# A graph layer on one core: PE's sums in two banks by turns, half of its signals taken out, and two bias rows moved off PE

## The chip, the cores and the metric

The kernel runs on one core of a Trainium2 chip. The metric is the device time of one execution in microseconds (us): the median of three runs. Engines are named as in the profile: PE (matmul), PEld (its weight loads), DVE (vector), ACT (scalar), POOL (GpSimd), SP (sync, which here only issues DMAs).

## What is computed

One message-passing layer over 6250 nodes (128 features) and 100000 edges sorted by destination, with H = 256 hidden columns:

```
h    = relu(concat(x[src], x[dst]) @ Wm1 + bm1)
h    = relu(h @ Wm2 + bm2)
agg  = segment_sum(h @ Wm3 + bm3, dst) / clip(count, 1)
upd  = relu(concat(x, agg) @ Wn1 + bn1) @ Wn2 + bn2
out  = layernorm(x + x + upd)
```

The kernel keeps near float32 accuracy by splitting an operand into a high and a low part ("hi", "lo") and multiplying the parts separately.

## The kernel before, in words

**Opening stage** (up to about 90 us). For each of 13 groups of four windows (a window is 128 nodes), PE transposes x (L1066) and multiplies it by the two halves of Wm1 (L1084) and by half of Wn1 (L1105). A one-row matmul (L1078) puts the bias bm1 into the bank of the first product. ACT copies the first product (table a, L555) and the high half of the second (table b, L562); DVE makes b's low half (L836). ACT adds bn1 to one half of the Wn1 product (L566) and DVE to the other (L841). DVE works out from the edges the words and flags that steer the loop (L741 to L795), each a row of 392 numbers. Both tables go to DRAM.

**Edge loop** (about 95 to 1358 us). The 391 blocks of 256 edges run four to a body (U = 4); bodies 0, 1 and the last are written out, the others are a hardware loop on each engine. Step k of the program holds work on several blocks, in this order on each engine:

- POOL: two gathers of 128 rows of table a for block k + 4 or so (L510), each an indirect DMA. They wait until PE has freed the buffer four blocks back: the signal s_ta, which PE gives with the last transpose (L1163).
- SP: loads of b_win (rows of table b) and rel, behind s_ex.
- PE: four transposes of the gathered rows (L1163), two matmuls that expand b into the same bank (L1129, signal s_ex), the four matmuls that sum block k - 5 into its window (sum_segments, L1142 and L1144, signal s_sg), and the twelve of the second layer for block k - 2 (L1194, signal s_w2). These are four signals a block.
- ACT: relu of the second layer of block k - 3 (L592, behind s_w2), relu of the first layer of block k (L597, behind s_ex), and the bias bm2 into the second layer's bank (L600).
- DVE: the low half of the second layer of block k - 3 (L932), a step signal s_clr (L941), the low half of the first layer of block k (L944), the one-hot matrix for the sums of block k - 3 (L873), and that for the expansion of block k + 2 (L858).

The low halves gate PE: the transposes of block k wait for L944 of block k - 2 and so do the L1194 of step k; the sums of block k - 5 wait for its L932, its one-hot, and s_clr. The engines' waits on signals are tested in program order by the sequencer of the engine.

All blocks of a window are summed in one bank, SUM. Where a window ends, finish_sums (L888) on DVE waits for s_sg, adds the bank to agg (L886) and zeroes it (L893) ahead of that step's s_clr. A block that spans two windows has a second sum, in the bank SUM_MORE, from a further one-hot that DVE makes a step before; finish_further (L898) adds it to agg. With these inputs the profile shows 97 additions to agg: 49 windows and 48 blocks that span two. Flags and words in memory tell each engine where that is.

**Final stage** (about 1358 to 1458 us). For each group, PE transposes the means (L1212, L1213), makes the hidden product (L1223, L1227), puts bn2 into the bank by a one-row matmul (L1235) and adds the update (L1240). DVE computes 2x + update (L991) and the statistics of the normalisation; ACT scales (L640). x is loaded again in threes ahead.

## Time and profile before

| | |
|---|---|
| median of 3 runs | 1459.47 us (1455.62 to 1460.34) |
| the profiled execution's own time | 1460.04 us |
| its span, first to last instruction | 1458.2 us |
| mean granted TensorE clock | 0.974 |
| PE, PEld busy | 88%, 83% of the span |
| DVE, ACT, POOL busy | 67%, 51%, 53% |
| DMA | 145 GB/s over the span |

The page of the profile gives busy shares, the chain of work that ended last, and groups of instructions with the idle time ahead of each and what ended it. "issue" and "remote" are endings for which the profile saw no instruction that had just finished: in the second, a signal came from somewhere long after its instruction was done. The timeline lists instructions in order of time, like ones merged (x4 is four), with the idle time of the engine before and its releaser in brackets. The last matmul of a merged row starts well before the row's modelled end.

### The profile page before, as it was taken

To read this page: it belongs to the slowest core of one execution; us is meant where nothing else is said; L and a number is where in the kernel's file an instruction comes from. 1 tells how busy PE (TensorE), PEld (TensorE's weight loads), DVE (VectorE), ACT (ScalarE), POOL (GpSimd) and SP (SyncE) were. 2 spreads that over 40 slices of the span, in tenths; PEclk is the share of its full clock that TensorE was granted. 3 is DMA by queue.
4 is the path that set the end of the run, shared out by engine and by line. 5 is a ranking of instruction groups with operands and counts; after the bars stand their busy time and mean duration, and the time that the engine had idled before them with its cause. 6 is when DMAs were issued, how large, how long until landed. Compare 5 with 4: busy or idle time off the path is not lost.

```text
span 1458.2 us, 37162 instructions
## 1 busy us (share of the span) xinstructions
PE 1278.1 (88%) x9807; PEld 1205.2 (83%) x9808; DVE 976.7 (67%) x2120; ACT 746.7 (51%) x1409; POOL 778.1 (53%) x810
## 2 busy tenths in 40 slices
PE   7969889898988888899888889898889988899797
PEld 6758788887988888888888888888888888888686
DVE  5746666666666666666676667767777777777575
ACT  4525544555454545455454455555455554545486
POOL 1156666666665666656666565666565655654000
PEclk9989999999999999989999999999999999999899
DMA  9854444444444444445454444455544444544023
GB/s 285 288 194 143 143 148 147 147 143 143 146 148 142 143 146 147 140 141 146 141 144 147 134 147 144 139 145 147 143 140 146 146 137 147 146 129 134 8 59 90
DMA packets 158504, 211.26 MB, mean 145 GB/s; under 512 B 24234, under 2 KB 127106, under 8 KB 158467
## 3 DMA queue, kind: packets, MB, share of 16 engines
q1 hardware_dynamic: 119818, 107.51, 25.6%
q0 software_dynamic: 37536, 102.55, 22.6%
q10 hardware_dynamic: 1112, 0.79, 0.2%
q8 instruction: 13, 0.21, 0.1%
q14 instruction: 25, 0.20, 0.0%
HBM read 187.96 MB, written 22.80 MB: 145 GB/s over the span
## 4 chain that ended last, share of the span: by engine, by line
PE 55%; issue 17%; another core or an unknown queue 7%; DVE 7%; ACT 6%; DVEq 6%; DMA 1%; ACTq 0%; POOL 0%
PE bank L1194 23%; PE bank L1129 7%; PE bank L1163 6%; PE bank L1142 5%; PE bank L1144 4%; DVEq L323 3%; PE bank L1227 2%; PE bank L1084 2%; DVE onehot L873 2%; ACT h L597 2%; ACT h_hi L592 2%; ACT bank L600 2%; PE bank L1240 1%; PE bank L1105 1%
## 5 line engine op out<-in xcount | busy, mean ns | idle before, releaser
L510 POOL DMA_INDIRECT a_edge<-a_table,src_idx x782 | 759.8, 972 | 499.5 <-remote 193.5
L1194 PE MATMUL bank<-w,h 128*128 128x256 f32 x4692 | 642.3, 285 | 24.2 <-issue 23.8
L1194 PEld LDWEIGHTS bank<-w,h 128*128 128x128 f32 x4692 | 597.8, 192 | 31.9 <-issue 31.7
L592 ACT ACTIVATE h_hi<-bank 128x512 fp32r<-128x512 f32 x391 | 235.4, 602 | 388.5 <-remote 195.3
L932 DVE SCALAR_TENSOR_TENSOR h_lo<-bank,h_hi 128x512 fp32r<-128x512 f32 x391 | 267.5, 684 | 178.7 <-issue 125.0
L944 DVE SCALAR_TENSOR_TENSOR h<-bank,h 128x512 fp32r<-128x512 f32 x391 | 268.8, 687 | 158.6 <-issue 98.9
L597 ACT ACTIVATE h<-bank 128x512 fp32r<-128x512 f32 x391 | 233.4, 597 | 244.1 <-PE bank L1129 115.1
L1142 PE MATMUL bank<-h_hi,onehot 128*128 128x258 f32 x878 | 244.3, 299 | 95.6 <-DVE onehot L873 40.6
L1142 PEld LDWEIGHTS bank<-h_hi,onehot 128*128 128x128 f32 x878 | 168.1, 192 | 121.0 <-issue 71.1
L1163 PE MATMUL bank<-ident,a_edge 128*128 128x128 f32 x1564 | 242.5, 278 | 18.1 <-issue 10.7
L600 ACT COPY bank<-b_bc 128x512 f32<-128x512 f32 x391 | 234.0, 598 | 0.0
L1144 PE MATMUL bank<-h_lo,onehot 128*128 128x256 f32 x878 | 231.3, 284 | 0.0
L873 DVE SCALAR_TENSOR_TENSOR onehot<-iota,first_node,dst_col 128x256 fp32r<-128x256 int16 x439 | 209.5, 477 | 7.3 <-issue 3.1
L1163 PEld LDWEIGHTS bank<-ident,a_edge 128*128 128x128 f32 x1564 | 184.0, 142 | 24.9 <-issue 16.2
L1129 PE MATMUL bank<-onehot_t,b_win 128*128 128x256 f32 x782 | 191.7, 327 | 10.4 <-issue 6.3
L858 DVE TENSOR_SCALAR onehot_t<-rel,node_half 128x256 fp32r<-128x256 int16 x391 | 146.4, 375 | 36.7 <-issue 17.6
L1144 PEld LDWEIGHTS bank<-h_lo,onehot 128*128 128x128 f32 x878 | 167.9, 191 | 0.0
L1129 PEld LDWEIGHTS bank<-onehot_t,b_win 128*128 128x128 f32 x782 | 120.2, 194 | 24.5 <-issue 14.3
L886 DVE TENSOR_TENSOR agg<-bank,agg 128x258 f32 x97 | 41.4, 427 | 25.5 <-issue 12.4
L1084 PEld LDWEIGHTS bank<-h,h_lo 128*128 128x128 f32 x294 | 40.1, 199 | 1.2
L1084 PE MATMUL bank<-h,h_lo 128*128 128x256 f32 x294 | 40.4, 289 | 0.0
L500 POOL MEMSET agg<- 128x12642 f32 x1 | 10.7, 10676 | 54.6 <-DVE flags_dve L793 54.6
(142 smaller groups left out, 551.7 us busy)
## 6 DMA issues: line engine op xcount, KB each, us to landing
b_win<-b_table SPq DMA_DIRECT2D x391, 128.0 KB
rel<-rel_dram SPq DMA_DIRECT2D x196, 128.0 KB
a_edge<-a_table,src_idx POOLq DMA_INDIRECT x782
a_table<-work SPq DMA_DIRECT2D x12, 512.0 KB, 3.4
b_table<-work SPq DMA_DIRECT2D x4, 1024.0 KB, 5.4
b_table<-h SPq DMA_DIRECT2D x4, 1024.0 KB, 5.2
b_table<-a_edge SPq DMA_DIRECT2D x4, 1024.0 KB, 5.0
f_x<-in_x SPq DMA_DIRECT2D x12, 256.0 KB, 5.4
```

The lines of the kernel that those rows point to most:

```text
L510: pool.indirect_dma_start(a_edge[:, b % R * TB + t, :], None, a_table, bass.IndirectOffsetOnAxis(ap=src_idx[:, b * TB + t:b * TB + t + 1], ...
L592: act.activation(h2_hi[:, (k - AHEAD - 1) % U, :, 0:H], bank[H2[(k - AHEAD - 1) % U]][:, :].rearrange("p (t h) -> p t h", t=TB), ACT.Relu) ...
L597: act.activation(h1[:, k % U, 0, :], bank[k % 2][:, :], ACT.Relu).then_inc(s_h1h, 1)
L600: act.copy(bank[H2[k % U]][:, :], b2_bc[:, :, :].rearrange("p t h -> p (t h)")).then_inc(s_seed, 1)
L873: dve.scalar_tensor_tensor(onehot[:, slot, :, :], iota16[:, :, :], first_node[:, bass.ds(w, 1)], dst_col[:, bass.ds(i * (U * TB) + k * TB, ...
L932: dve.scalar_tensor_tensor(h2_lo[:, j, :, :], bank[H2[j]][:, :].rearrange("p (t h) -> p t h", t=TB), 0.0, h2_hi[:, j, :, 0:H].bitcast(F32) ...
L944: dve.scalar_tensor_tensor(h1[:, k % U, 1, :], bank[k % 2][:, :], 0.0, h1[:, k % U, 0, :].bitcast(F32), ALU.max, ALU.subtract).then_inc(s_ ...
L1129: ins = pe.matmul(bank[k % 2][:, h * EB:(h + 1) * EB], rows[:, h * P:(h + 1) * P], hot, start=False, stop=True, skip_group_check=True)
L1142: pe.matmul(to[:, 0:HC], onehot[:, slot, t, :], h2_hi[:, k % U, t, :], start=(start and t == 0), stop=False, skip_group_check=True)
L1144: ins = pe.matmul(to[:, 0:H], onehot[:, slot, t, :], h2_lo[:, k % U, t, :], start=False, stop=(t == TB - 1), skip_group_check=True)
L1163: ins = pe.matmul(bank[k % 2][:, h * EB + t * P:h * EB + (t + 1) * P], a_edge[:, k % R * TB + t, h * P:(h + 1) * P], ident[:, :], start=(t ...
L1194: ins = pe.matmul(to, h1[:, j, a, h * EB + t * P:h * EB + (t + 1) * P], w2[:, b, h, :], start=False, stop=(a == 1 and h == KH - 1), skip_g ...
```

## The change

It has these parts.

1. **Signals of PE.** s_ta is gone: POOL's gathers wait for s_ex, which PE gives after the two L1129. s_sg is gone from the step: what waited for the sums waits for s_w2 of the same step. Two signals a block are left, s_ex and s_w2. s_clr of DVE is gone as well, and PE's wait for it.
2. **Two banks for the sums.** Both lie in one tensor, sums, and a register on PE and on DVE holds which is the own bank and which the other. The second sum of a block that spans two windows goes into the other bank with start=True, and the banks change roles; DVE adds the old bank to agg once, with no zeroing. PE waits there for s_fin of the window before. The cases that this doesn't cover (a window that ends with a block, a block over three windows) take a longer way, with s_sg; here that is only the last block.
3. **Order on DVE.** The one-hot for the sums stands ahead of L932's work, the one-hot for block k + 2 ahead of L944's, behind the wait for ACT; the flag is tested once a step, and the further one-hot is made two steps before its use in place of one.
4. **Opening stage.** bm1 is loaded to all partitions and DVE adds it where it moves table a from the bank (in place of ACT's copy and of PE's L1078); ACT adds bn1 to both halves. The words have a few more rows of arithmetic on DVE.
5. **Final stage.** bn2 is loaded to all partitions, POOL makes x + bn2 and adds x, and DVE adds that to the update. L1235 is gone.

```diff
-        bank = [ctx.enter_context(nc.psum_tensor(f"bank{i}", [P, 512], F32)) for i in range(8)]
-        SUM, SUM_MORE = 4, 5
+        bank = [ctx.enter_context(nc.psum_tensor(f"bank{i}", [P, 512], F32)) for i in range(4)]
+        sums = ctx.enter_context(nc.psum_tensor("sums", [P, 1024], F32))
+        bank += [sums[:, 0:512], sums[:, 512:1024]]
+        bank += [ctx.enter_context(nc.psum_tensor(f"bank{i}", [P, 512], F32)) for i in range(6, 8)]
+        SUM = 4
...
-                    pool.wait_ge(s_ta, b - R + 1)
+                    pool.wait_ge(s_ex, b - R + 1)
...
+            pool.wait_ge(s_fb, 16)
+            for g in range(NG):
+                n = size(g)
+                pool.wait_ge(s_xr[g % 3], 16 * (g // 3 + 1) + (16 if g == NG - 1 and n > 1 else 0))
+                if g:
+                    pool.wait_ge(s_fxb, g)
+                pool.tensor_tensor(x_bn2[:, 0:n, :], x_res[:, g % 3, 0:n, :],
+                                   bn2_bc[:, :].unsqueeze(1).to_broadcast([P, n, D]), ALU.add).then_inc(s_fxa, 1)
+                pool.wait_ge(s_fxa, g + 1)
+                pool.tensor_tensor(x_res[:, g % 3, 0:n, :], x_res[:, g % 3, 0:n, :], x_bn2[:, 0:n, :], ALU.add
+                                   ).then_inc(s_fxb, 1)
...
-                    act.activation(hx[0][:, (g - 1) * GW * P:((g - 1) * GW + n) * P], bank[6][:, 0:n * P],
-                                   ACT.Identity, bias=bn1_col[:, 0:1]).then_inc(s_hxa, 1)
+                    for h, to in enumerate((hx[0], hx_more)):
+                        act.activation(to[:, (g - 1) * GW * P:((g - 1) * GW + n) * P], bank[6 + h][:, 0:n * P],
+                                       ACT.Identity, bias=bn1_col[:, h:h + 1]).then_inc(s_hxa, 1)
...
-            dve.tensor_tensor(rows_lo[0:2, :], rows_in[0:2, :], rows_hi[0:2, :], ALU.subtract
-                              ).then_inc(s_lo, 1)
-            dve.wait_ge(s_lo, 1)
...
+                    dve.wait_ge(s_ab, pair(g - 1, q))
+                    if g >= 3 and q == 0:
+                        dve.wait_ge(s_as[(g - 1) % 2], (g - 1) // 2 * 16)
+                    dve.tensor_tensor(a_out[:, (g - 1) % 2, 2 * q:2 * q + m, :],
+                                      bank[2 + q][:, 0:m * H].rearrange("p (w h) -> p w h", h=H),
+                                      b1_bc.unsqueeze(1).to_broadcast([P, m, H]), ALU.add
+                                      ).then_inc(s_ac, 1)
...
             def make_further_onehot(i, k, j):
+                dve.wait_ge(s_sgm, more)
                 dve.reg_add(more, more, 1)
                 make_onehot(FURTHER, i, k, j, s_ohm)
...
+            def end_window(i, k, word):
 
                 w = word & 63
+                with dve.If((word & (3 * 2**6)) > 0):
+                    with dve.If((word & 2**7) > 0):
+
+                        dve.wait_ge(s_w2, i * U + (k + BACK - AHEAD + 1))
+                        add_sums(own, within(w, 0, NW - 1))
+                        dve.reg_mov(swap, own)
+                        dve.reg_mov(own, other)
+                        dve.reg_mov(other, swap)
+                    with dve.If((word & 2**6) > 0):
+                        dve.reg_add(left, left, 1)
+                        dve.wait_ge(s_sg, left)
+                        add_sums(own, within(w, 0, NW - 1))
+                        dve.wait_ge(s_add, added)
+                        no_row = ident[:, 0:1].to_broadcast([P, HC])
+                        dve.tensor_tensor(bank_at(own), no_row, no_row, ALU.subtract
+                                          ).then_inc(s_add, 1)
+                        dve.reg_add(added, added, 1)
+                        further = (word >> 15) & 63
+                        with dve.If(further > 0):
+                            with dve.Fori(1, within(further, 1, NW - 1) + 1) as j:
+                                make_further_onehot(i, k, j)
+                                dve.wait_ge(s_sgm, more)
+                                dve.wait_ge(s_add, added)
+                                add_sums(other, within(w + j, 1, NW - 1))
...
+                        make_onehot(j, i, k - AHEAD - 1, 0, s_oh)
                         dve.wait_ge(s_h2h, i * U + (k - AHEAD))
                         dve.scalar_tensor_tensor(h2_lo[:, j, :, :],
                                                  bank[H2[j]][:, :].rearrange("p (t h) -> p t h", t=TB),
                                                  0.0, h2_hi[:, j, :, 0:H].bitcast(F32),
                                                  ALU.max, ALU.subtract).then_inc(s_h2l, 1)
+                    if there(i, k):
+                        dve.wait_ge(s_h1h, i * U + (k + 1))
+                        if there(i, k + 2):
+                            if (k + 2) % 2 == 0:
+                                dve.wait_ge(s_rc[(k + 2) // 2 % RC], (i + (k + 2) // U) * 16 + 16)
+                            make_onehot_t(k + 2)
+                        dve.scalar_tensor_tensor(h1[:, k % U, 1, :], bank[k % 2][:, :], 0.0,
+                                                 h1[:, k % U, 0, :].bitcast(F32), ALU.max, ALU.subtract
+                                                 ).then_inc(s_h1l, 1)
                     with dve.If(flag > 0):
                         word = load_words(dve, words_dve, i * U + k, 1, DVE_TOP)[0]
                         if there(i, k - BACK):
-                            with dve.If((word & 64) > 0):
-                                finish_sums(i, k - BACK, word)
-                    dve.nop().then_inc(s_clr, 1)
-                    if there(i, k):
-                        dve.wait_ge(s_h1h, i * U + (k + 1))
-                        dve.scalar_tensor_tensor(h1[:, k % U, 1, :], bank[k % 2][:, :], 0.0,
-                                                 h1[:, k % U, 0, :].bitcast(F32), ALU.max, ALU.subtract
-                                                 ).then_inc(s_h1l, 1)
-                    if there(i, k - AHEAD - 1):
-                        make_onehot((k - AHEAD - 1) % U, i, k - AHEAD - 1, 0, s_oh)
-                    with dve.If(flag > 0):
-                        word = load_words(dve, words_dve, i * U + k, 1, DVE_TOP)[0]
-                        if there(i, k - BACK):
-                            finish_further(i, k - BACK, word)
-                        if there(i, k - BACK + 1):
-                            with dve.If(word > 2**20 - 1):
-                                make_further_onehot(i, k - BACK + 1, 1)
+                            end_window(i, k - BACK, word)
+                        if there(i, k - AHEAD - 1):
+                            with dve.If(word > 2**21 - 1):
+                                make_further_onehot(i, k - AHEAD - 1, 1)
                         if there(i, k) and there(i, k + 1):
-                            with dve.If((word & (127 * 2**7)) > 0):
+                            with dve.If((word & (127 * 2**8)) > 0):
                                 far_onehots_t(k + 1, word)
-                    if there(i, k) and there(i, k + 2):
-                        if (k + 2) % 2 == 0:
-                            dve.wait_ge(s_rc[(k + 2) // 2 % RC], (i + (k + 2) // U) * 16 + 16)
-                        make_onehot_t(k + 2)
...
+                    dve.wait_ge(s_fxb, g - 2)
                     y = f_y(g - 3)
-                    dve.scalar_tensor_tensor(y.rearrange("p (w d) -> p w d", d=D), x_res[:, (g - 3) % 3, 0:n, :], 2.0,
-                                             bank[F_UPD][:, 0:n * D].rearrange("p (w d) -> p w d", d=D),
-                                             ALU.mult, ALU.add).then_inc(s_fy, 1)
+                    dve.tensor_tensor(y.rearrange("p (w d) -> p w d", d=D),
+                                      bank[F_UPD][:, 0:n * D].rearrange("p (w d) -> p w d", d=D),
+                                      x_res[:, (g - 3) % 3, 0:n, :], ALU.add).then_inc(s_fy, 1)
...
-                    pe.matmul(bank[4 + q][:, 0:m * H], ones2[:, :], b1_rows[:, 0:m * H], start=True, stop=False,
-                              skip_group_check=True)
...
+            def end_window(k, word):
+
+                with pe.If(word > 2**13 - 1):
+
+                    pe.wait_ge(s_fin, ended)
+                    pe.reg_add(ended, ended, 1)
+                    with pe.If((word & 2**13) > 0):
+
+                        pe.matmul(bank_at(other)[:, 0:2], ident[:, :], ident[:, 0:2], start=True, stop=True,
+                                  skip_group_check=True).then_inc(s_sg, 1)
+                    further = (word >> 7) & 63
+                    with pe.If(further > 0):
+                        with pe.Fori(1, within(further, 1, NW - 1) + 1):
+                            pe.reg_add(more, more, 1)
+                            pe.wait_ge(s_ohm, more)
+                            sum_segments(bank_at(other), FURTHER, k, True).then_inc(s_sgm, 1)
+                    with pe.If(word > 2**14 - 1):
+                        pe.reg_mov(swap, own)
+                        pe.reg_mov(own, other)
+                        pe.reg_mov(other, swap)
+                    with pe.If((word & 2**13) > 0):
+
+                        pe.wait_ge(s_fin, ended)
...
-                        ins.then_inc(s_ta, 1)
...
-                        pe.wait_ge(s_clr, i * U + k)
-                        sum_segments(bank[SUM], (k - BACK) % U, k - BACK, False).then_inc(s_sg, 1)
+                        ins = sum_segments(bank_at(own), (k - BACK) % U, k - BACK, False)
+                        if not there(i, k - AHEAD):
+                            ins.then_inc(s_w2, 1)
                         with pe.If(flag > 0):
-                            word = load_words(pe, words_pe, i * U + k, 1, PE_TOP)[0]
-                            with pe.If(word > 127):
-                                with pe.Fori(1, within(word >> 7, 1, NW - 1) + 1):
-                                    sum_further(k - BACK)
+                            end_window(k - BACK, load_words(pe, words_pe, i * U + k, 1, PE_TOP)[0])
...
-                    pe.matmul(bank[F_UPD][:, 0:n * D].rearrange("p (w d) -> p w d", d=D), ones2[:, :],
-                              bn2_rows[:, :].unsqueeze(1).to_broadcast([P, n, D]), start=True, stop=False,
-                              skip_group_check=True)
```

**PE, in the step of the hardware loop**, from the wait for the expansion's operands to the test of the flag (s_step_of_sums_done is s_clr). Before:

```order
L1173 REGISTER_ALU
L1129 MATMUL bank<-onehot_t,b_win 128x256 [waits s_b_win_loaded0,s_onehot_t_made]
L1129 MATMUL bank<-onehot_t,b_win 128x256
L1177 REGISTER_ALU
L1142 MATMUL bank<-h_hi,onehot 128x258 [waits s_step_of_sums_done,s_onehot_made,s_h2_lo]
L1144 MATMUL bank<-h_lo,onehot 128x256
L1142 MATMUL bank<-h_hi,onehot 128x258
L1144 MATMUL bank<-h_lo,onehot 128x256
L1181 COMPARE_AND_BRANCH
L323 ISA
```

and with the change:

```order
L1219 REGISTER_ALU
L1153 MATMUL bank<-onehot_t,b_win 128x256 [waits s_b_win_loaded0,s_onehot_t_made]
L1153 MATMUL bank<-onehot_t,b_win 128x256
L1223 REGISTER_ALU
L1166 ISA [waits s_onehot_made,s_h2_lo]
L1170 MATMUL sums<-h_hi,onehot 128x258
L1172 MATMUL sums<-h_lo,onehot 128x256
L1170 MATMUL sums<-h_hi,onehot 128x258
L1172 MATMUL sums<-h_lo,onehot 128x256
L1228 COMPARE_AND_BRANCH
L322 ISA
L322 TENSOR_LOAD words_pe
```

The wait for the step signal is gone and the bank is addressed by a register. The loop's body on PE is longer by what the flag guards, which a step without a window's end jumps over.

**DVE, in the same loop.** Before, two places of a step: behind the flag's first test, and from the end of the step into the next one:

```order
L943 REGISTER_ALU
L944 SCALAR_TENSOR_TENSOR h<-bank,h 128x512 [waits s_h1_hi]
L873 ISA
L873 SCALAR_TENSOR_TENSOR onehot<-iota,first_node,dst_col 128x256
L949 COMPARE_AND_BRANCH
```

```order
L961 ISA
L858 TENSOR_SCALAR onehot_t<-rel,node_half 128x256 [waits s_rel_loaded1]
L931 REGISTER_ALU
L932 SCALAR_TENSOR_TENSOR h_lo<-bank,h_hi 128x512 [waits s_h2_hi]
L936 REGISTER_ALU
L936 COMPARE_AND_BRANCH
L323 ISA
```

and with the change, from the start of the body's first step:

```order
L891 ISA
L891 SCALAR_TENSOR_TENSOR onehot<-iota,first_node,dst_col 128x256
L960 REGISTER_ALU
L961 SCALAR_TENSOR_TENSOR h_lo<-bank,h_hi 128x512 [waits s_h2_hi]
L966 REGISTER_ALU
L969 ISA [waits s_h1_hi]
L876 TENSOR_SCALAR onehot_t<-rel,node_half 128x256 [waits s_rel_loaded1]
L971 SCALAR_TENSOR_TENSOR h<-bank,h 128x512
L974 REGISTER_ALU
L974 COMPARE_AND_BRANCH
```

Both one-hots moved ahead of the low halves that follow them; L891 is the one-hot for the sums, L961 the low half of the second layer, L876 the one-hot for block k + 2, L971 the low half of the first layer.

## Rows read from the trace of the kernel before

**Rows 1.** Windows of the three stages: us, busy by engine (instructions), PEclk, DMA share, GB/s

```profile
0.00:90.00 90.00, 72.41 (x475) 64.15 (x476) 60.11 (x111) 44.83 (x82) 17.25 (x26) 1.00 0.86 276
95.60:1345.05 1249.45, 1110.04 (x8725) 1057.31 (x8725) 846.21 (x1739) 631.00 (x1167) 756.23 (x779) 0.98 0.48 144
1358.00:1458.20 100.20, 86.13 (x538) 75.24 (x538) 61.53 (x252) 67.39 (x154) 0.00 (x0) 0.91 0.21 57
```

**Rows 2.** Timeline, PE in the loop, step starts with and without a stall

```profile
199.78 0.65 PE L1163 MATMUL bank<-ident,a_edge 128*128 128x128 f32 x4 [0.29 <-issue]
...
212.31 0.65 PE L1163 MATMUL bank<-ident,a_edge 128*128 128x128 f32 x4 [0.26 <-issue]
```

**Rows 3.** The same view later in the loop

```profile
277.90 0.60 PE L1163 MATMUL bank<-ident,a_edge 128*128 128x128 f32 x4
...
280.48 0.60 PE L1163 MATMUL bank<-ident,a_edge 128*128 128x128 f32 x4
```

**Rows 4.** Timeline of all engines in one step of the loop

```profile
208.20 0.60 PE L1163 MATMUL bank<-ident,a_edge 128*128 128x128 f32 x4
...
209.36 0.87 PE L1194 MATMUL bank<-w,h 128*128 128x256 f32 x6
...
211.20 0.85 PE L1194 MATMUL bank<-w,h 128*128 128x256 f32 x5 [0.44 <-issue]
211.36 0.60 ACT L592 ACTIVATE h_hi<-bank 128x512 fp32r<-128x512 f32 x1 [1.21 <-remote]
...
211.66 0.95 POOL L510 DMA_INDIRECT a_edge<-a_table,src_idx  x1 [1.50 <-remote]
```

**Rows 5.** Timeline, the opening stage, where POOL issues no gathers

```profile
21.78 1.56 PE L1105 MATMUL bank<-h_lo,onehot_t 128*128 128x512 f32 x6
...
23.38 0.69 ACT L566 ACTIVATE f_x<-bank,bn_col 128x512 f32<-128x512 f32 x1 [0.33 <-PE bank L1105]
```

**Rows 6.** Timeline of POOL in the loop

```profile
200.37 0.95 POOL L510 DMA_INDIRECT a_edge<-a_table,src_idx  x1 [0.31 <-issue]
202.24 0.95 POOL L510 DMA_INDIRECT a_edge<-a_table,src_idx  x1 [0.93 <-remote]
...
205.44 0.95 POOL L510 DMA_INDIRECT a_edge<-a_table,src_idx  x1 [0.83 <-remote]
...
209.20 0.95 POOL L510 DMA_INDIRECT a_edge<-a_table,src_idx  x1 [0.30 <-issue]
```

**Rows 7.** Who waited for whom: us in total, times, longest

```profile
ACT h_hi L592 <- remote: 195.3, 118, 4.7
...
PE bank L1142 <- DVE onehot L873: 40.6, 37, 2.6
...
PE bank L1142 <- DVEq L941: 24.7, 44, 1.9
```

**Rows 8.** Timeline of PE where a block spans two windows

```profile
292.42 0.39 PE L1142 MATMUL bank<-h_hi,onehot 128*128 128x258 f32 x1 [0.67 <-DVE onehot L873]
```

**Rows 9.** The page's DMA queues: packets, MB, share of 16 engines

```profile
q8 instruction: 13, 0.21, 0.1%
```

**Rows 10.** Groups by line and form: busy us, mean ns | idle before

```profile
L944 DVE SCALAR_TENSOR_TENSOR h<-bank,h 128x512 fp32r<-128x512 f32 x391 | 268.8, 687 | 158.6 <-issue 98.9 <-ACT h L597 49.1 <-DVE bank L893 8.8
...
L858 DVE TENSOR_SCALAR onehot_t<-rel,node_half 128x256 fp32r<-128x256 int16 x391 | 146.4, 375 | 36.7 <-issue 17.6 <-DVE agg L886 13.0 <-DMA rel<-rel_dram 6.1
...
L491 POOL CAST agg<-a_edge 98x1024 f32<-98x1024 int32 x1 | 1.0, 1041 | 5.2 <-DMA a_edge<-in_src 5.2
```

**Rows 11.** Timeline of PE at the opening stage

```profile
20.13 0.39 PE L1078 MATMUL bank<-b_rows,ones 128*128 128x512 f32 x1
20.36 1.58 PE L1084 MATMUL bank<-h,h_lo 128*128 128x256 f32 x12
```

**Rows 12.** Timeline of PE in the final stage

```profile
1390.42 0.39 PE L1235 MATMUL bank<-bn_rows,ones 128*128 128x512 f32 x1
1390.65 1.95 PE L1240 MATMUL bank<-wn,agg 128*128 128x128 f32 x16
```

173 lines of the change are left out of this document (77 added, 96 removed).

## Prediction

> **What bounds the kernel now.** I read the windows of the three stages first [rows 1]: the loop holds 1249.4 of 1458.2 us, from the first transposes of block 0 to those of block 390. That is 390 steps of 3.20 us. In this stage PE is busy 89% and its clock is granted at 0.98 of full speed, so neither the clock nor missing work explains the pace. The timeline of PE says what a step needs: where nothing holds it, transposes follow transposes after 280.48 - 277.90 = 2.58 us [rows 3]. But in a body of four steps far from any window's end it takes 212.31 - 199.78 = 12.53 us, 3.13 a step [rows 2]. So 0.55 us a step is lost without a window's end, and that is the larger loss (390 x 0.55 = 215 us of the 244 above the pace of 2.58).
>
> The reader is to see where it goes in rows 4. PE starts its transposes at 208.20, so the twelve L1194 of the step before were issued by then. ACT's L592 waits for those alone and sits idle 1.21 us, yet it starts at 211.36: the signal came some 3.1 us late. POOL's gather at 211.66 waits for the transposes of 208.20, which lasted 0.60, and is idle 1.50: that signal came some 2.8 us late. Both arrive within 0.3 us of one another. And PE itself halts 0.44 us in the middle of its twelve L1194, for nothing that the profile shows. In the opening stage, where POOL issues no gathers, the same kind of signal takes 0.04 us (21.78 + 1.56 to 23.38) [rows 5]. My reading: **while POOL issues gathers, PE's signals queue up, pass one by one, and come out together once POOL has been idle for a while.** The waits put down to "remote" are this: 195.3 us on L592 alone [rows 7]. The timeline of POOL gives the clockwork [rows 6]: a gather follows the last after 1.25 us (205.44 to 209.20 is three of them); after the second of a pair POOL stands 202.24 - 200.37 = 1.87 us until PE's signal gets through. A block's pair thus costs 1.25 + 1.87 = 3.12 us. Where two pairs run on, the release takes longer, 211.66 - 209.20 = 2.46, and the two blocks cost 6.22, 3.11 each. That is the pace of rows 2: **POOL waits for a signal that its own gathers hold back**, and behind the same queue ACT, DVE and then PE stand.
>
> Second, the windows' ends: PE waits 40.6 us for the further one-hot and 24.7 us for the step signal behind DVE's zeroing [rows 7], 65.3 us together.
>
> **The change part by part.**
>
> *Two signals of PE a block in place of four.* The gathers still cost 2.50 us a block, below PE's 2.58. What changes is the queue: half as many signals wait in it, so that s_ex, which POOL needs, is sooner at its head. If the release then takes 1.87 us but comes once per two pairs, two blocks cost 3 x 1.25 + 1.87 = 5.62, 2.81 a block; once per three pairs, 8.12, 2.71. With no help at all it stays one release per pair, 3.12. No row shows two signals a block beside gathers, so these are the bounds: 2.58 (PE alone) and 3.12. I take 2.81, as halving the signals should at least double the run that they can sustain.
> The Trainium skill's page "TensorE: Matmul & The Clock Gate" (The cost: per-tile semaphore tail) prices an increment at about 26 ns, so by it 2 x 391 increments are worth 20 us at most. Rows 4 and 5 put 0.04 us against about 3 us, by whether POOL gathers; where they differ the rows decide.
>
> *s_ex for s_ta.* POOL's trigger comes later by the two L1129, some 0.3 us of 2.58; it costs nothing while POOL is not behind PE by its four buffers, 4 x 2.58 us. If that cover were gone, 0.3 a block, inside the bounds above.
>
> *s_clr gone, order on DVE.* PE's wait for it vanishes. L944's work now stands behind the one-hot of 0.375 us (L858's) [rows 10]. The chain from transposes to the transposes two blocks on is: expansion over after about 0.8, the signal, ACT 0.60, DVE 0.375 + 0.69, hand-offs 0.3, so 2.8 us and the signal's delay, against 2 x 2.85. A delay up to 2.9 is covered. DVE's work a step is 0.69 + 0.69 + 0.48 + 0.375 = 2.2 us, covered by 2.85, though not by much.
>
> *Two banks.* The 65.3 us of waits go. What stays at each of the 48 blocks over two windows is four matmuls, 4 x 0.12 = 0.48 (0.12 from the six L1194 in 0.87 [rows 4]), and the time in which PE's sequencer reads the word and branches; nearest is the gap of 0.67 [rows 8], of which I keep 0.7. PE alone then needs 2.58 + 48/390 x 1.18 = 2.73 a step. DVE's wait for s_w2 at a window's end has the low half of the next step behind it, but that waits for the same signal. Late next is that addition of 0.43 us ahead of it. The limits 2.81 and 2.73 lie so close that each will show now and then: I take **2.85**. Loop: 390 x 2.85 = 1111.5, so -137.9.
>
> *The longer body on PE.* It grows by about a fifth, in rows that the flag jumps over. The Trainium skill's page "Runtime: NRT & Kernel Launch" (Instruction fetch mechanics) says a taken branch whose target is outside the current two pages forces a fetch. The page of the profile has only 13 packets on one instruction queue in all [rows 9], against 98 bodies, so the loop isn't fetched again each time, and I price this at nothing; by the rule it is rival 5.
>
> *Opening stage.* PE loses 24 L1078 at 20.36 - 20.13 = 0.23 [rows 11]: -5.5. ACT's second half of the Wn1 product, 0.69 [rows 5], stands ahead of PE at the four groups where PE shares the banks and at the end: 5 x 0.69 = +3.4. DVE's new additions (24 at 0.69 for 12 at 0.74) and words lie beside PE, as DVE is busy 60 of 90 us [rows 1]; with that cover gone they cost up to 8. Net -2.1.
>
> *Final stage.* 12 L1235 at 1390.65 - 1390.42 = 0.23: -2.8 [rows 12]. POOL's two additions a group of 512 columns: nearest is its cast of 1024 columns in 1.04 us [rows 10], so 1 to 2 us a group against 100.2 / 13 = 7.7, and POOL has nothing else there [rows 1]: nothing. With that cover gone, 26.
>
> Sum on the profiled execution's 1460.0: -137.9 - 2.1 - 2.8 = -142.8, **1317 us**. The median of the runs is 0.6 lower, nothing at this size.
>
> **Rivals.**
> 1. *PE alone decides.* The queue never matters again: 2.73 a step, 1065, so -184.7 and -4.9: **1270**. For it: stretches at 2.58 exist already [rows 3]. Against it: POOL's 2.50 a block leave no idle time in which a queue would empty. 0.15.
> 2. *The pace stays with one release per pair.* 3.12 a step: 1216.8, -32.6 - 4.9: **1423**. For it: runs of one and of two pairs cost the same now. Against it: the late signal of rows 4 had others ahead of it that are gone. 0.12.
> 3. *The number of signals is no matter*, only the windows' ends gain: -65.3 - 4.9: **1390**. 0.08. By the Trainium skill's price of an increment (the first page named above) it would be 20 us less, 1370.
> 4. *Slower.* As in 2, and DVE at each window's end stands at s_w2 with its addition (0.43), the next one-hot (0.48) and hand-offs (0.1) ahead of the low half on which PE waits. With cover it is nothing; it decides if the signals stay about 3 us late, since PE's chain then has no slack: 48 x 1.0 on 1423 gives **1471**. For it: ACT's late signal. Against: half of the signals. 0.03.
> 5. *PE's longer loop is fetched anew in each body.* The 13 packets took 0.1% of 16 engines' span, 23 us, so 1.8 each; one exposed in each of 98 bodies is 176 us on the forecast: **1493**. Against it: the loop of before is no longer than a fifth below and shows none [rows 9]. 0.03. This is what the rule of the Trainium skill on taken branches would do here.
>
> That the change doesn't do what it says, so that s_w2 comes as often as before with something else in the queue, I give 0.01, at no change.
>
> **How the numbers follow.** The forecast has 0.58. The range of 8 in 10 takes in it, rivals 1 and 3 and the bounds of the opening stage: 1260 to 1398; rivals 2, 4 and 5 and the last stay out with 0.19. A measurement of this kernel can tell about 0.3%, 4 us (the runs shown lie that far apart). Faster: 0.58 + 0.15 + 0.12 + 0.08 = 0.93; within 0.3%: 0.01; slower: 0.06.
>
> **What would show it.** Right: "remote" on ACT's second-layer relu falls to under half of 195 us; POOL's gathers run in runs of four and more at 1.25 us, with a release of about 1.9 after them; steps of PE mostly at 2.58 with one longer in two or three; no halts inside the twelve; the waits of 40.6 and 24.7 gone; 24 and 12 one-row matmuls gone and the groups of the final stage 0.23 apart less. Wrong: POOL still in pairs 3.1 apart (rival 2), or "remote" as large as before with a faster loop. If DVE's low half becomes what PE waits for with signals prompt, then I misjudged the order on DVE.

## The result, and the profile after

The changed kernel takes 1477.24 us (median of 4 runs, 1473.80 to 1482.74) against 1459.12 for the kernel before: a ratio of 1.0132, 95% interval 1.0092 to 1.0172. It is slower by 1.3%; 1317 us and a gain of 10% were forecast. The profiled execution took 1479.83 us, with a span of 1478.0 and a mean granted clock of 0.963 (0.974 before). A run more than 1.5% above the fastest of its kernel is left out of every ratio below; there is one, in e6.

The windows of the changed kernel by stage come first (columns as in [rows 1]): up to the first transposes of block 0, from there to those of block 390, and the rest.

```profile
0.00:100.97 100.97, 70.05 (x450) 61.57 (x451) 66.93 (x123) 39.21 (x69) 20.08 (x26) 0.95 0.81 255
100.97:1367.26 1266.29, 1128.25 (x8724) 1075.19 (x8725) 807.18 (x1648) 619.32 (x1167) 748.28 (x779) 0.97 0.48 142
1367.26:1478.00 110.74, 91.55 (x599) 80.85 (x597) 73.82 (x266) 70.73 (x160) 32.55 (x28) 0.91 0.19 52
```

The loop starts 5.4 us later than before (100.97 against 95.60), takes 16.8 us more (1266.3 against 1249.45, 3.25 a step in place of 3.20), and what follows it is 2.4 us shorter (110.7 against 1458.2 - 1345.05 = 113.15). The three make the 19.8 us between the spans.

Within the loop PE's busy time grows by 18.2 us (1128.25 against 1110.04 in [rows 1]) with the same matmuls (8724 and 8725 recorded), and its idle time shrinks by 1.4 (138.0 against 139.4). The trace's own record of the clock has 79.6 us of this loop at the lower of the two levels, 53.7 of the one before. More on this below.

Who waited for whom (in total, times, longest), of the same view as [rows 7]:

```profile
ACT h_hi L599 <- remote: 337.2, 116, 6.0
POOL a_edge L511 <- remote: 196.0, 150, 2.7
...
DVE agg L909 <- PE bank L1238: 87.7, 41, 3.6
...
PE sums L1170 <- issue: 58.2, 47, 2.0
```

L599 is what L592 was. Its wait for signals that come long after their instruction was to fall to under half of 195.3 us; it rose to 337.2. PE's waits of 40.6 and 24.7 us at the windows' ends are gone, and one of 58.2 us stands in their place, 47 times 1.24 us, in which the profile sees PE wait for nothing (of that kind there were 28.8 us, 33 times, before). DVE, idle 25.5 us ahead of its additions before, is so for 95.9 us, of which 87.7 are this wait.

POOL's gathers, far from any end, answer to [rows 6]:

```profile
203.50 0.95 POOL L511 DMA_INDIRECT a_edge<-a_table,src_idx  x1 [1.51 <-remote]
204.75 0.94 POOL L511 DMA_INDIRECT a_edge<-a_table,src_idx  x1 [0.30 <-issue]
206.00 0.95 POOL L511 DMA_INDIRECT a_edge<-a_table,src_idx  x1 [0.30 <-issue]
207.25 0.95 POOL L511 DMA_INDIRECT a_edge<-a_table,src_idx  x1 [0.30 <-issue]
209.80 0.94 POOL L511 DMA_INDIRECT a_edge<-a_table,src_idx  x1 [1.61 <-remote]
```

Here they run in fours, as forecast. Counted from 130 us on, the runs of four went from 44 to 116 and the runs of two from 275 to 134. But two blocks take 209.80 - 203.50 = 6.30 us, 3.15 each: the pair of before took 3.12. The release comes 209.80 - 207.25 = 2.55 us after the start of the last gather, not 1.87. The medians say the same of both kernels: 1.93 and 1.92 us after a run of two, 2.46 and 2.52 after a run of four. And ACT and PE at the same place:

```profile
209.34 0.59 PE L1238 MATMUL bank<-w,h 128*128 128x256 f32 x3 [0.47 <-issue]
209.49 0.60 ACT L599 ACTIVATE h_hi<-bank 128x512 fp32r<-128x512 f32 x1 [3.24 <-remote]
```

PE still halts inside its twelve second-layer matmuls (0.31 us before this row, 0.47 at it). The program has no wait there. Over the loop such halts come to 52.3 us (111 of them), against 24.2 us (49) before. And ACT's relu, idle 3.24 us, starts 0.31 us ahead of POOL's gather: one burst of signals again, now once per four gathers.

### The profile page after: what moved, and what is told of

It reads as the page before. It is cut to its first block, busy times and chain, and to the rows that moved or that the text cites. A ratio compares the mean times of both kernels' runs of the same rounds, so it can differ in the third digit from the quotient of the medians.

```text
span 1478.0 us, 36599 instructions
## 1 busy us (share of the span) xinstructions
PE 1289.8 (87%) x9771; PEld 1217.6 (82%) x9772; DVE 947.9 (64%) x2036; ACT 729.3 (49%) x1396; POOL 800.9 (54%) x832
## 4 chain that ended last, share of the span: by engine, by line
PE 81%; issue 10%; DVE 3%; DMA 2%; SPq 2%; ACT 1%; another core or an unknown queue 1%; DVEq 0%; POOL 0%; ACTq 0%
PE bank L1238 40%; PE bank L1210 12%; PE sums L1170 8%; PE bank L1153 7%; PE sums L1172 7%; PE bank L1271 2%; PE sums L1281 1%; PE bank L1256 1%; SPq L366 1%; DMA a_table<-work 1%; PE bank L1102 0%; DMA mm_dram<-agg 0%; PE sums L1257 0%; PE sums L1102 0%
## 5 line engine op out<-in xcount | busy, mean ns | idle before, releaser
L511 POOL DMA_INDIRECT a_edge<-a_table,src_idx x782 | 752.1, 962 | 525.4 <-remote 196.0
L1238 PE MATMUL bank<-w,h 128*128 128x256 f32 x4692 | 667.1, 289 | 60.9 <-issue 58.1
L1238 PEld LDWEIGHTS bank<-w,h 128*128 128x128 f32 x4692 | 609.5, 194 | 81.7 <-issue 80.5
L599 ACT ACTIVATE h_hi<-bank 128x512 fp32r<-128x512 f32 x391 | 235.0, 601 | 505.5 <-remote 337.2
L961 DVE SCALAR_TENSOR_TENSOR h_lo<-bank,h_hi 128x512 fp32r<-128x512 f32 x391 | 267.9, 685 | 233.3 <-issue 209.3
L1170 PE MATMUL sums<-h_hi,onehot 128*128 128x258 f32 x878 | 244.8, 300 | 60.5 <-issue 58.2
L971 DVE SCALAR_TENSOR_TENSOR h<-bank,h 128x512 fp32r<-128x512 f32 x391 | 266.1, 681 | 0.0
L891 DVE SCALAR_TENSOR_TENSOR onehot<-iota,first_node,dst_col 128x256 fp32r<-128x256 int16 x439 | 208.4, 481 | 64.0 <-issue 44.6
L1172 PE MATMUL sums<-h_lo,onehot 128*128 128x256 f32 x878 | 230.3, 283 | 0.0
L1170 PEld LDWEIGHTS sums<-h_hi,onehot 128*128 128x128 f32 x878 | 167.9, 191 | 74.3 <-issue 70.2
L876 DVE TENSOR_SCALAR onehot_t<-rel,node_half 128x256 fp32r<-128x256 int16 x391 | 149.3, 382 | 76.6 <-DMA rel<-rel_dram 43.6
L1172 PEld LDWEIGHTS sums<-h_lo,onehot 128*128 128x128 f32 x878 | 167.3, 191 | 0.0
L909 DVE TENSOR_TENSOR agg<-sums,agg x49 | 20.9, 427 | 95.9 <-PE bank L1238 87.7
L524 POOL TENSOR_TENSOR work<-work 128x512 f32<-128x512 f32 (+1 forms) x13 | 15.7, 1210 | 61.6 <-DMA work<-in_x 61.3
L1102 PE MATMUL bank<-h,h_lo 128*128 128x256 f32 x147 | 28.7, 309 | 9.3 <-DVE h L851 6.0
```

Source lines behind the costliest of these rows:

```text
L511: pool.indirect_dma_start(a_edge[:, b % R * TB + t, :], None, a_table, bass.IndirectOffsetOnAxis(ap=src_idx[:, b * TB + t:b * TB + t + 1], ...
L599: act.activation(h2_hi[:, (k - AHEAD - 1) % U, :, 0:H], bank[H2[(k - AHEAD - 1) % U]][:, :].rearrange("p (t h) -> p t h", t=TB), ACT.Relu) ...
L891: dve.scalar_tensor_tensor(onehot[:, slot, :, :], iota16[:, :, :], first_node[:, bass.ds(w, 1)], dst_col[:, bass.ds(i * (U * TB) + k * TB, ...
L961: dve.scalar_tensor_tensor(h2_lo[:, j, :, :], bank[H2[j]][:, :].rearrange("p (t h) -> p t h", t=TB), 0.0, h2_hi[:, j, :, 0:H].bitcast(F32) ...
L971: dve.scalar_tensor_tensor(h1[:, k % U, 1, :], bank[k % 2][:, :], 0.0, h1[:, k % U, 0, :].bitcast(F32), ALU.max, ALU.subtract).then_inc(s_ ...
L1170: pe.matmul(to[:, 0:HC], onehot[:, slot, t, :], h2_hi[:, k % U, t, :], start=(start and t == 0), stop=False, skip_group_check=True)
```

## The experiments

Four theories. **A**: POOL's gathers hold PE's signals back, and the pace follows from that whatever the number of signals. **B**: the number of signals sets the delay. **D**: DVE, standing at s_w2 at a window's end with the next step's work behind it, makes the step over an end long. **S**: PE's own instruction stream there (the word, branches, register arithmetic) does. "A step over an end" is below the step in which PE sums a block of two windows; there are 48 such blocks, and the mean lengths given are over the 47 among blocks 0 to 384, worked out from the starts of each block's first transposes in the trace. Far from an end a body of four steps is given, as in [rows 2]. The kernel before was run beside each on the same chip, and every ratio is to that. The changed kernel was not run on every one of these chips; between chips only ratios are compared.

### The number of signals: four, and one

e2 gives PE the two signals again, with nobody waiting for them:

```diff
+                        ins.then_inc(s_ta, 1)
...
-                        if not there(i, k - AHEAD):
-                            ins.then_inc(s_w2, 1)
+                        if not there(i, k - AHEAD):
+                            ins.then_inc(s_w2, 1)
+                        else:
+                            ins.then_inc(s_sgx, 1)
```

> The changed kernel with two more signals of PE a block, behind the transposes and behind the sums, for which nobody waits; so again four a block. Theory A (POOL's gathers hold PE's signals back as long as they run, and what comes out comes out together, so the number is no matter): a body of four steps far from a window's end stays at 12.5 us and the time within 10 us of 1477. Theory B (the number of signals in the queue sets the delay, and the change gained by it what it lost elsewhere): body of four steps 13 us or more, time 1500 or more.

Measured: 1452.35 us beside 1439.40 for the kernel before, 1.0090 (1.0055 to 1.0124). The body of blocks 32 to 35 takes 12.4 us. Theory B is refuted: with twice the signals the kernel is, if anything, nearer to the one before (1.0090 against 1.0132, with intervals that overlap). Nor do the signals set the length of POOL's runs: e2 has 114 runs of four and 139 of two, as the changed kernel has. What made the runs longer was not isolated; POOL waits for s_ex in both.

e6 goes the other way, to one signal a block (for the loop; the last three blocks keep s_w2), and DVE's addition waits for s_sgm:

```diff
-                        act.wait_ge(s_w2, i * U + (k - AHEAD))
+                        if there(i, k):
+                            act.wait_ge(s_ex, i * U + (k + 1))
+                        else:
+                            act.wait_ge(s_w2, i * U + (k - AHEAD) - (NBE - 3))
...
-                        ins.then_inc(s_w2, 1)
+                        if isinstance(i, int) and i * U + k - AHEAD >= NBE - 3:
+                            ins.then_inc(s_w2, 1)
```

> The changed kernel with one signal of PE a block, behind the expansion; ACT's second-layer relu waits for it too, in place of the signal behind the second layer, and DVE's addition at a window's end waits for the signal of the further sums, which is 1.5 us earlier. Theory A (number no matter): body of four steps 12.5 us, the time lower by what DVE's earlier addition brings, 0 to 20 us: 1457 to 1477. Theory B (number matters): one signal a block is below what passes between two gathers, the body falls to 11.2 us or less, the time to 1370 or less.

Measured: 1462.31 us in the median of three runs (1451.97 to 1469.83), 1.0162 (1.0111 to 1.0213). The profile is of a fourth, which took 1476.42: body 12.2 us, L602 (the same relu) idle 301.8 us by "remote". One signal a block comes as late as two or four. The count does not set the pace. (1.0162 is 1483 us on the scale of the case's own chip, above what either theory had expected. The profile has a lower mean clock, 0.956, with 97.3 us of its loop at the lower level against 45.9 in e2; why was not pursued.)

### The gathers halved

e3 takes every second gather away:

```diff
-                for t in range(TB):
-                    pool.indirect_dma_start(a_edge[:, b % R * TB + t, :], None, a_table,
+                pool.indirect_dma_start(a_edge[:, b % R * TB, :], None, a_table,
...
+                        sp.dma_start(a_edge[:, k % R * TB + 1, :], a_table[0:P, :]).then_inc(s_g[k % R * TB + 1], 16)
```

> The changed kernel with one gather a block in place of two; the second tile's rows are the first 128 of table a, loaded by SyncE with a plain transfer (that part of the result is left out: those edges use other rows). Theory A (the gathers hold PE's signals back and this sets the pace of 3.12 us a step): with POOL busy 1.25 of 2.6 us the signals come through in its idle time; a body of four steps far from a window's end takes 10.3 to 10.8 us, 'remote' on ACT's second-layer relu falls from 337 to under 80 us, the time to 1270 to 1330. Rival C (the pace is set by PE's own instruction stream or by the order on DVE, and the late signals are only a sign of it): the body stays at 12 us or more and the time above 1430.

Measured: 1302.46 us, 0.9048 (0.9016 to 0.9079), as theory A says. In e3's list of waits "remote" does not occur at all; the same relu has

```profile
ACT h_hi L599 <- PE bank L1238: 399.3, 387, 3.1
...
PE sums L1170 <- issue: 28.9, 47, 1.1
```

that is, each wait ends as the second layer ends. The body is 10.3 us, 2.58 a step, with nothing changed on PE, DVE and ACT. Theory C of the expectation falls, and the halts inside the twelve are gone too (none in the loop). What in a gather does it, its issuing on POOL or its indirect transfer, e3 does not tell: it takes both away and leaves a plain transfer of as many rows. A step over an end still takes 4.35 us on average, 1.77 above the others, with no signal late.

### DVE at a window's end

e7 lets the addition wait for the further sums' signal:

```diff
-                        dve.wait_ge(s_w2, i * U + (k + BACK - AHEAD + 1))
+                        dve.wait_ge(s_sgm, more)
```

> The changed kernel, but at a window's end DVE's addition waits for the signal of the further sums (which PE gives at each of the 48 blocks anyway) and not for s_w2 of that step, which comes 12 matmuls (1.5 us) later. Theory D (DVE standing at s_w2 with the next step's work behind it, 87.7 us in all, is what makes a crossing step longer than before): the crossing steps fall from 5.8 us by up to 1.0, the time by 10 to 45 us, to 1435 to 1465 on the scale of the first measurement. Theory S (PE's own instruction stream at a crossing, reading the word, branches, register addresses, is what makes it long): crossing steps stay within 0.3 us, the time within 8 us of the changed kernel.

e5 is the changed kernel on the same chip:

> The changed kernel itself, on the chip of the runs beside it, so that they can be compared with it. The ratio to the kernel before should be 1.013 again (1.009 to 1.017).

Measured: e5 1476.00 us beside 1459.95, 1.0129 (1.0089 to 1.0169); e7 1487.16, 1.0198 (1.0164 to 1.0233). The steps over an end take 5.81 us in e5 and 5.89 in e7. DVE's wait at the addition did fall, in e5 and then e7:

```profile
DVE agg L909 <- PE bank L1238: 81.1, 38, 3.5
```

```profile
DVE agg L909 <- remote: 49.1, 20, 2.6
DVE agg L909 <- issue: 9.5, 26, 0.5
```

The step over an end did not. Theory D is refuted, and rival 4 of the prediction with it as a mechanism; e14 below bears it out where signals are prompt. That e7 stays within 8 us, as theory S had it, does not hold either. Why e7 is 11 us above e5 stays open: its profiled execution has a span of 1476.4, only 3.7 above e5's 1472.7.

### The order on DVE

e9 puts DVE's order back (the two one-hots behind the low halves, the one for block k + 2 last):

```diff
-                        make_onehot(j, i, k - AHEAD - 1, 0, s_oh)
                         dve.wait_ge(s_h2h, i * U + (k - AHEAD))
...
-                            make_onehot_t(k + 2)
...
+                    if there(i, k - AHEAD - 1):
+                        make_onehot((k - AHEAD - 1) % U, i, k - AHEAD - 1, 0, s_oh)
                     with dve.If(flag > 0):
...
+                        make_onehot_t(k + 2)
```

> The changed kernel with DVE's order of before: h2's low half, h1's low half, the one-hot for the sums, the window's end, the one-hot for block k + 2 last. Theory O (the one-hot for block k + 2, 0.35 us and its waits for the rel rows, 43.6 us, stands ahead of the low half on which PE waits): the time falls by 10 to 45 us, to 1430 to 1467 on the scale on which the changed kernel has 1477, and body and crossing steps are shorter. Theory A (DVE has its input late and in bursts, since PE's signals are, so the order inside is no matter): within 8 us.

Measured: 1301.18 us, and this beside a kernel before of **1253.14** us: 1.0391 (1.0375 to 1.0407). The four runs e8, e9, e12 and e13 were made together on another chip, and there the kernel before takes 13 to 14% less than in the three sets of runs so far (1459, 1439 and 1460). The order itself is worth nothing there: on a further chip with a kernel before at 1252.34 the changed kernel measures

> The changed kernel once more, as the reference of the two runs beside it. On a chip where PE's signals come at once: first block at 99 to 101 us, steps 2.57, crossing steps 4.3, ratio about 1.03 to 1.04 to the kernel before (48 x 1.2 for the crossings and 4 for the opening, on 1253). On a chip where they come late: ratio 1.013.

1301.60 us, 1.0385 (1.0367 to 1.0402), the same as e9. With late signals the order was not tried.

### Sets of runs with and without late signals

What the later sets lack is the late signals. "The first kind" and "the second kind" of chip stand below for sets of runs with and without them. That the chip itself makes the difference is not shown: the three sets with late signals were made first, the four without them after, and no chip on record was met in both conditions. One chip, that of e8 and e9, was met again 13 minutes later with e18, and had prompt signals both times.

 The waits of the changed kernel there (run e6b_after):

```profile
ACT h_hi L599 <- PE bank L1238: 399.1, 389, 3.1
...
DVE agg L909 <- PE bank L1238: 107.1, 48, 2.6
...
PE sums L1170 <- issue: 28.4, 47, 1.1
```

No wait in its list is put down to "remote". With all 782 gathers it runs as e3 did with half of them: 2.58 a step, 4.34 over an end, no halt inside the twelve, and its loop

```profile
101.30:1189.10 1087.80, 1048.83 (x8720) 1028.55 (x8721) 819.39 (x1647) 655.78 (x1167) 755.87 (x779) 1.00 0.56 166
```

takes about 1088 us. That the gathers are harmless there was tried on the kernel before, with e3's edit:

> The kernel before with one gather a block, as in the run e3 (the second tile's rows are the first 128 of table a by a plain transfer; that part of the result is left out). Theory A: steps far from an end take 2.58 here too, so the four signals of before are no burden once POOL has idle time; the time is 0.90 to 0.93 of the kernel before, and the difference to e3's 0.905 is what the change's two banks are worth at the 48 ends with prompt signals: by the 65.3 us of waits up to 0.04, by e3's 4.35 us a crossing step, of which 1.8 above the pace, less. Theory B (four signals are a burden of their own): steps far from an end stay above 2.8, the ratio above 0.95.

Measured: 1250.13 us, 0.9981 (0.9971 to 0.9990). Half the gathers bring 3 us on this kind of chip; on the other they brought the changed kernel some 11% (0.9048 against 1.0132). So the expectation's reading (a ratio of 0.90 to 0.93) fails, because it was written for the first kind, while its second half stands: four signals a block are no burden, steps far from an end are 2.58 here.

e8 leaves out all work at the ends:

```diff
-                            end_window(i, k - BACK, word)
-                        if there(i, k - AHEAD - 1):
-                            with dve.If(word > 2**21 - 1):
-                                make_further_onehot(i, k - AHEAD - 1, 1)
...
-                        with pe.If(flag > 0):
-                            end_window(k - BACK, load_words(pe, words_pe, i * U + k, 1, PE_TOP)[0])
```

> The changed kernel with nothing done at a window's end: no further sums and no swap on PE, no addition to agg and no further one-hot on DVE (so the sums per node and all that follows from them in the result are left out); the words are read and the flags tested no more. If the pace far from the ends, 3.12 us a step, is set by the gathers alone, the loop is 390 x 3.12 = 1217 us and the time 101 + 1217 + 111 = 1429, so the 48 ends cost the changed kernel 48 us net and the kernel before 32. If instead the ends are what holds the rest back (the queue would settle into another pattern without them), the steps far from an end get faster or slower by over 0.1 us and the time is below 1390 or above 1460.

Measured: 1216.28 us, 0.9716 (0.9701 to 0.9731), on the second kind of chip, so its numbers for 3.12 a step can't be read there. Against e9 and e6b (1301) the ends cost the changed kernel 85 us, 48 x 1.77; the kernel before, 37 us above e8 at 1253, pays about 0.8 for each (by the loops of e13 and e8, 1042.3 and 1007.4 us, 0.7). **Here the change's loss lies bare: 49 us, at the windows' ends and in the opening, not in the signals.** The loops of e6b_after and e13 differ by 46 of them.

### PE's instruction stream at an end

A step over an end on the second kind of chip, first in the changed kernel (e6b_after, PE): own sums, further sums, second layer, next transposes.

```profile
261.44 0.28 PE L1172 MATMUL sums<-h_lo,onehot 128*128 128x256 f32 x1
262.19 0.38 PE L1170 MATMUL sums<-h_hi,onehot 128*128 128x258 f32 x1 [0.47 <-issue]
...
262.65 0.28 PE L1172 MATMUL sums<-h_lo,onehot 128*128 128x256 f32 x1
263.15 1.67 PE L1238 MATMUL bank<-w,h 128*128 128x256 f32 x12 [0.22 <-DVE h L971]
264.65 0.60 PE L1210 MATMUL bank<-ident,a_edge 128*128 128x128 f32 x4
```

Then in the kernel before (e13_before_half, PE):

```profile
254.00 0.28 PE L1144 MATMUL bank<-h_lo,onehot 128*128 128x256 f32 x1
254.12 0.38 PE L1142 MATMUL bank<-h_hi,onehot 128*128 128x258 f32 x1
...
254.58 0.28 PE L1144 MATMUL bank<-h_lo,onehot 128*128 128x256 f32 x1
254.69 1.59 PE L1194 MATMUL bank<-w,h 128*128 128x256 f32 x12
256.12 0.60 PE L1163 MATMUL bank<-ident,a_edge 128*128 128x128 f32 x4
```

From the last of the own sums to the first of the further ones it is 262.19 - 261.44 = 0.75 us in the one and 254.12 - 254.00 = 0.12 in the other; from the last further one to the second layer 0.50 and 0.11. The kernel before reads its word and branches within the time that its matmuls take anyway; the changed one does not. (Of the 0.50 the profile puts 0.22 down to DVE's low half, L971.)

e10 moves the end behind the second layer in the changed kernel, e11 does so in the kernel before:

```diff
-                        with pe.If(flag > 0):
-                            end_window(k - BACK, load_words(pe, words_pe, i * U + k, 1, PE_TOP)[0])
...
                         ins.then_inc(s_w2, 1)
+                    if there(i, k - BACK):
+                        with pe.If(flag > 0):
+                            end_window(k - BACK, load_words(pe, words_pe, i * U + k, 1, PE_TOP)[0])
```

> The changed kernel, but PE's work at a window's end (the word read, the branches, the further sums, the swap) stands behind the twelve L1238 of the step in place of ahead of them. Theory S (PE's instruction stream): reading and branching can then run while the matmuls issued before are still being worked off, so of the 1.24 us that PE stands ahead of the further sums and the 1.2 behind them at least half goes; crossing steps 5.8 to 4.6 or less, the time down by 15 to 50 us. Theory D: nothing changes for DVE (it waits for s_w2, given before the further sums now as then), the time stays within 8 us. Third, PE's stream does not run ahead of its matmuls at all: the gaps only move, time within 8 us, with the gaps now ahead of the next transposes.

> The kernel before with the same move: its further sums, with the word and the branches ahead of them, stand behind the twelve L1194. Beside what it saves of PE's stream (as in the run before, 0 to 1.2 us a crossing step), the further one-hot has 1.5 us more to arrive, which takes most of the 40.6 us that PE waited for it. So 10 to 45 us less than the kernel before, 1395 to 1430 where that has 1439, if either matters; within 4 us of it if the pace of POOL's gathers takes back what a crossing step saves.

Measured, on the chip of e5 with late signals: e10 1474.68 us, 1.0124 (1.0078 to 1.0170), level with e5's 1.0129; e11 1457.12, 0.9989 (0.9970 to 1.0007), level with the kernel before. PE's idle time ahead of the sums falls from 59.1 in e5 to 11.9 us in e10 and comes up elsewhere (33.8 ahead of the transposes, 9.9 in e5). The step over an end takes 4.92 us in e10 in place of 5.81, but the one after it 3.33 in place of 2.78; in e11 it is 3.94 in place of 4.93 and 4.00 in place of 3.18. So with late signals the next step takes back more than half of what a step over an end saves, and both are inconclusive on theory S.

e14 gives the common end a straight path:

```diff
-                with pe.If(word > 2**13 - 1):
-
-                    pe.wait_ge(s_fin, ended)
-                    pe.reg_add(ended, ended, 1)
-                    with pe.If((word & 2**13) > 0):
+                with pe.If(word > 2**14 - 1):
+                    pe.wait_ge(s_fin, ended)
+                    pe.reg_add(ended, ended, 1)
+                    pe.reg_add(more, more, 1)
+                    pe.wait_ge(s_ohm, more)
+                    sum_segments(bank_at(other), FURTHER, k, True).then_inc(s_sgm, 1)
+                    pe.reg_mov(swap, own)
+                    pe.reg_mov(own, other)
+                    pe.reg_mov(other, swap)
+                with pe.If((word & 2**13) > 0):
+                    pe.wait_ge(s_fin, ended)
+                    pe.reg_add(ended, ended, 1)
```

> The changed kernel with a straight path on PE for the ends that all but the last block take: behind the flag and the word, one branch, then the waits, the four further matmuls and the swap, without the test for the longer way, the loop over further windows and the second test. Same computation. Theory S (PE's instruction stream at an end sets the crossing step): crossing steps shorter by 0.4 to 0.8 us, on a chip with prompt signals 20 to 38 us less than the changed kernel; on one with late signals, where the gathers' pace takes back part, 0 to 20 us. Rival (it is the addressing by register in the sums' matmuls, or the four matmuls themselves): within 0.2 us a crossing step, within 8 us.

Measured, beside e6b_after: **1250.73 us, 0.9982 (0.9973 to 0.9992)**, 50.9 us less than the changed kernel. That is more than theory S had forecast (20 to 38), since a step over an end fell by 1.16 us, from 4.34 to 3.18, and not by 0.4 to 0.8. The pages give the count of executed instructions, e6b_after first, then e14:

```profile
span 1300.1 us, 36599 instructions
```

```profile
span 1249.9 us, 36164 instructions
```

435 fewer, 9 at each of the 48 ends (4 compare-and-branch, 4 of register arithmetic, 1 move), save 1.06 us an end. The same place in e14 has no gap left, and the step takes 267.28 - 264.18 = 3.10 us:

```profile
264.18 0.60 PE L1210 MATMUL bank<-ident,a_edge 128*128 128x128 f32 x4
...
265.22 0.28 PE L1172 MATMUL sums<-h_lo,onehot 128*128 128x256 f32 x1
265.34 0.28 PE L1170 MATMUL sums<-h_hi,onehot 128*128 128x258 f32 x1
...
265.81 1.63 PE L1238 MATMUL bank<-w,h 128*128 128x256 f32 x12
267.28 0.60 PE L1210 MATMUL bank<-ident,a_edge 128*128 128x128 f32 x4
```

Theory S is shown, for the second kind of chip. The rival (register addresses, the four matmuls) falls: both are still there. So does theory D once more: DVE's addition still waits for s_w2. Whether it is the number of the instructions or one sort of them, the branches above all, was not separated, and neither e14 nor e15 met late signals.

e15 has the edits of e14 and of e10 together.

> As e14, and PE's part of a window's end behind the twelve L1238 of the step. If PE's stream runs ahead while the twelve are worked off (the kernel before shows no gap at its further sums on the chip with prompt signals), crossing steps fall to 3.1 to 3.4 us there, 45 to 55 us less than the changed kernel, and the kernel is level with the one before but for the opening's 4 us and the final stage's 3; on a chip with late signals 0 to 30 us less. If the stream cannot run ahead, the same as e14.

Measured: 1248.96 us, 0.9976 (0.9967 to 0.9986), and again in two more sets of runs, e16 and e18:

> The kernel of run e15 on another chip. Prompt signals: ratio 0.9976 again. Late signals: the changed kernel's 1.013 less what the ends no longer cost. Net of the pace of 3.12 they cost it 48 x 1.03 = 49 us; if the shorter stay of PE counts in full, ratio 0.98; if the pace takes back all but what shows in the steps after an end, 0.99 to 1.01.

> The kernel of run e15 once more. Prompt signals (before at 1253): ratio 0.997. Late signals (before at 1440 to 1460): 0.98 if the shorter stay of PE counts in full, 0.99 to 1.01 if the gathers' pace takes it back.

1249.02 us, 0.9974 (0.9965 to 0.9983), and 1248.88, 0.9966 (0.9952 to 0.9980). All three met a kernel before at 1252 to 1253, so prompt signals. Beside e14 the move brings 1.8 us; a step over an end is 3.09 us in place of 3.18.

### The opening and the final stage

e1 is the kernel before with the parts 4 and 5 of the change (without the longer words) alone.

> The kernel before with only the opening and the final stage of the change (b1 added by DVE, both halves of the Wn1 product moved by ACT, bn2 added by POOL); the loop is that of before. Theory P (the stages add up as the two profiles show them): the loop starts 5.4 us later (100.97 against 95.61) and the part behind it is 2.4 us shorter, so 1459.1 + 5.4 - 2.4 = 1462 us, and the loop takes 1249 us as before. Rival Q (the later start comes from the longer words or from the way the loop begins, not from the opening's own edits): the loop starts at 96 or earlier, and the time is 1457 or less.

Measured: 1440.31 us, 1.0010 (0.9992 to 1.0028), on a chip with late signals. Its loop starts at 95.89 us, so the opening's own edits cost 0.3 where the changed kernel shows 5.4, and the time is 0.9 us above the kernel before. The interval of the ratio (-1.2 to +4.0 us) does not exclude theory P's 3, and does exclude rival Q's 2 less. So only the start of the loop speaks, and there rival Q holds. The start varies from run to run of one program, though: the kernels with the opening of before start their loops at 94.1 to 95.6 us, those with the changed one at 98.2 to 102.3 (99.14 in e5, the same kernel). So the 5.4 could as well be anything from 3 to 8; e1's single 95.89 lies just above the first group. DVE's rows say what the rest is: from the start of the first instruction of the words' second half to the next low half, in the changed kernel,

```profile
54.12 0.55 DVE L764 CUSTOM_DVE_ANT_0 words_pe<-words_pe,agg 1x784 uint16<-1x784 uint16 x1
...
58.87 0.67 DVE L833 TENSOR_TENSOR h_lo<-bank,h_lo 128x512 fp32r<-128x512 f32 x1
```

and in e1

```profile
53.56 0.54 DVE L756 CUSTOM_DVE_ANT_0 words_pe<-words_pe,agg 1x784 uint16<-1x784 uint16 x1
...
56.16 0.67 DVE L815 TENSOR_TENSOR h_lo<-bank,h_lo 128x512 fp32r<-128x512 f32 x1
```

4.75 us against 2.60, with DVE busy without a gap on both sides. PE's list of waits in the opening has the same 2.1 us, in the changed kernel

```profile
PE bank L1102 <- DVE h L851: 6.0, 2, 3.2
```

and in e1

```profile
PE bank L1074 <- DVE h L833: 3.9, 2, 3.2
```

That accounts for 2.1 of the 5.1 us between the two; the rest was not traced further.

e12 is the kernel before with bn2 on POOL (part 5) and e11's move; e17 repeats it beside e16.

> The kernel before with the two pieces that cost nothing in the runs so far: bn2 added by POOL in the final stage (b1 and the loop as before), and the further sums behind the twelve L1194. Expected 2.5 to 4 us less by the one (12 fewer matmuls of 0.23 us) and 0 to 4 by the other: ratio 0.995 to 0.998. If it is 1.000 or more, neither is worth anything.

> The kernel of run e12 on the same chip as e16. Prompt signals: ratio 0.998 again. Late signals: e11 gave 0.9989 for the one piece, and the final stage's 3 us are 0.002: 0.997.

Measured: 1250.97 us, 0.9979 (0.9970 to 0.9989), and 1250.83, 0.9983 (0.9974 to 0.9992). The final stage is the one part of the change that did what it was priced at: groups of L1281 start 1406.04 - 1399.69 = 6.35 us apart in the changed kernel, 6.58 before. e15 is the version that beats both kernels, the one before by 0.2 to 0.3%, where signals are prompt; how it does where they come late was not measured.

## Why the prediction was wrong, point by point

- **What bounds the kernel** was read rightly. "POOL waits for a signal that its own gathers hold back" is what e3 shows: half the gathers, no late signal, 2.58 a step.
- **Two signals in place of four, 2.81 a step, -137.9 us: this step failed.** The assumption was that "halving the signals should at least double the run that they can sustain" at a release of 1.87. The run did double in 116 cases; 134 runs stayed at two gathers. But a run of four has its own release, 2.55 after the last gather's start here and 2.46 before the change. Two blocks a burst cost 3 x 1.25 + 2.55 = 6.30 where one block a burst had cost 3.12. e2 (four signals) and e6 (one) show that the count has no part in it. Rival 2 had the pace right: 3.12. By which path the gathers hold PE up stays open: PE waits only 7.5 us in all for gathered rows, and it halts inside its twelve, where the program has no wait, 52.3 us with late signals and not at all in e3 and e6b_after.
- **The rows warned of it.** They had a run of two pairs with its release 2.46 after the last gather's start and 3.11 a block. I used the release of the short run for the long one, though [rows 4, 6] together give the long one's. The same pace for one pair and for two was there to be read as the rule.
- **Two banks, -65.3 us of waits: mis-sized.** The waits did go. Against them I set 0.67 for reading the word and branching from [rows 8]; that row's idle time is put down to DVE's one-hot, so it was not even a measure of branching, and it is a row of a code with one test and one loop behind the flag; the new code has four more tests there. Where nothing hides it a step over an end has 1.77 us above the others, in place of the 1.18 of the forecast, and 0.6 in the kernel before (e13). On the case's own chip that is 5.8 us a step over an end against 4.9, of which the other steps take back most (2.89 against 2.97): the loop's 16.8 us are 0.35 an end. That the added instructions cause these 16.8 us is argued from the other kind of chip; no run with late signals tested it. And the 65.3 us were themselves a child of the late signals: where they are prompt, e13 (the kernel before with half the gathers) has 1.1 and 5.0 us of them left.
- **Much of the 16.8 us goes with the clock.** The granted clock in the loop is 0.97 after and 0.98 before: 79.6 against 53.7 us of it are at the lower of the two levels, 1.2 GHz. If PE's work took twice as long there, the 25.9 us more would be worth up to 13 of the 16.8, which is an estimate. That the whole difference is in PE's busy time and none in its idle time agrees with it. The stretches follow the ends: the 18 that begin after 290 us each begin 2.0 to 5.4 us after the start of a step over an end, where PE stands for 1.24 us; such places are 13% of the loop's time. In e5, the same kernel, it is 69.3 us, and by the same estimate at most 8 of the 15 that its loop takes more.
- **DVE's order and DVE at s_w2**: priced at nothing, and e9 (on prompt signals) and e7 bear it out. s_ex for s_ta was not tried alone.
- **Opening, -2.1: wrong in sign**, +5.4. The edits to matmuls and copies come to +0.3 (e1), one profile each. The words, put down as lying beside PE, are on a DVE that is dense where they stand.
- **Final stage, -2.8**: -2.4 measured.
- **Rivals.** Rival 4 gave 1471 and is nearest to 1477, with the pace right and the mechanism of the ends wrong (DVE's wait is no cause, e7). Rival 5 is refuted: the page still has 13 packets on that instruction queue. Rival 3 fails, since the ends gained nothing. Rival 1's condition, a queue that never matters, was met on the second kind of chip: 1270 forecast, 1301.6 measured, of which the dearer ends (1.77 for 1.18, 48 times) are 28. Both of rival 4's conditions, late signals and a dearer end, had a chance of 0.03; that was too little, as the one was rival 2's and stood open.
- The Trainium skill's price in "TensorE: Matmul & The Clock Gate" (The cost: per-tile semaphore tail), some 26 ns an increment, would by an estimate of 782 x 26 ns have the two added signals of e2 cost 20 us, 0.014 of the time; e2's ratio is the lower one of the two. No run here shows a cost of that size.

## What to carry to other kernels

When a wait is set by a feedback (POOL waits for PE's signal, which POOL's work holds back), changing how often it occurs does not change its length in proportion: look in the trace for the longer run that already occurs, and read its release there. Code that runs only at rare steps is not free for touching registers alone: count the instructions that PE's stream must pass between two matmuls, and write the common case as one straight path. And compare a kernel with its predecessor on the same chip: here one chip said +1.3% and another +3.9%.

## What the runs showed of the hardware

- Two conditions that differ in one trait. In three sets of runs (kernel before at 1459, 1439 and 1460 us) PE's signals come up to 3 us late while POOL issues indirect transfers, however many signals there are; in four others, on three other chips (1252 to 1253 us), no wait is put down to a late signal, and the same program takes 13 to 14% less. What differs between them, the chip or something else, is not known.
- In the first condition PE also halts inside a row of twelve matmuls that has no wait in it: 111 times, 52.3 us, in the changed kernel's loop, and never in e3 (half the gathers) or e6b_after (prompt signals).
- There a gather that waits for PE's signal starts about 1.0 us after the end of a run of two gathers (1.93 - 0.95) and about 1.6 after the end of a run of four (207.25 + 0.95 to 209.80); with one signal of PE a block (e6) or four (e2) it is 0.9 and 1.5.
- PE's stream spent about 1.06 us less at an end with 9 register and branch instructions fewer, where no matmul hid them: 0.12 us each on average (e6b_after against e14).
- In the changed kernel's loop on the case's own chip the clock fell to its lower level 18 times after 290 us, each time 2.0 to 5.4 us after the start of a step over an end, in which PE stood 1.24 us on average.
